# Four graph layers over 32 batches on one core: first loads put in another order, weights split later, and new places for all stages

## The reference, cut to what matters

```
x = L0(x): q,k,v = x@Wq.T+bq, x@Wk.T+bk, x@Wv.T+bv       (8 heads)
           s = q.k/sqrt(32), -inf where adj + eye == 0
           x = layernorm(x + softmax(s) v @ Wo.T + bo)*gamma+beta
x = L1(x): q,k,v as above with its weights                (8 heads)
           s = q.k/sqrt(32) + a_i + c_j + log(adj+1e-9)
           x = x + softmax(s) v          (no output projection)
x = L2(x): f = x@W_fc+b ; logits = (f@w_q)_i + (f@w_k)_j  (one head)
           masked by adj, leaky relu, softmax, x = x + att @ f
x = L3(x): like L0 with log(max(adj,1e-8)) in place of the mask
```

## Time and profile before

| what | us |
|---|---|
| median of 3 runs | 1794.17 |
| the 3 runs | 1792.88 to 1796.88 |
| the profiled execution, whole | 1796.79 |
| its span, first to last instruction | 1795.0 |
| first group, layer 0, 8.1 to 141.8 us | 133.7 |
| second group, layer 0, 448.2 to 576.3 us | 128.1 |
| layers 1, 2, 3 of the second group | 117.0, 76.5, 112.0 |

### The profile page before, as it was taken

How to read it: one execution, slowest core, us unless ns; L and a number is a source line. 1 busy time by engine, 2 the same in 40 slices (tenths; PEclk the granted TensorE clock), 3 DMA queues, 4 the chain that set the end, 5 groups by cost and what they waited for, 6 DMA issues and landing times.

```text
span 1795.0 us, 53987 instructions
## 1 busy us (share of the span) xinstructions
PE 1684.0 (94%) x23308; PEld 1290.8 (72%) x23308; DVE 1371.3 (76%) x2556; ACT 1203.0 (67%) x1886; POOL 1330.2 (74%) x994
## 2 busy tenths in 40 slices
PE   4899999899999999889999999989999999998996
PEld 3677776787776777677777677767777777766874
DVE  2899777767699976776779987776778998777674
ACT  2567875467877786456877787546687778754675
POOL 3555799278977499638987759945898767992788
PEclk8999999999999999999999999999999999999998
DMA  7100010102121001100222100010123200101001
GB/s 217 43 19 19 16 29 25 36 14 66 55 89 49 18 15 37 31 19 19 74 82 66 37 19 20 27 47 7 31 73 94 61 19 14 32 25 36 14 26 42
DMA packets 76432, 74.79 MB, mean 42 GB/s; under 512 B 6562, under 2 KB 76196, under 8 KB 76196
## 3 DMA queue, kind: packets, MB, share of 16 engines
q1 hardware_dynamic: 75092, 70.55, 13.2%
q10 hardware_dynamic: 1104, 0.79, 0.1%
HBM read 62.93 MB, written 8.39 MB: 40 GB/s over the span
## 4 chain that ended last, share of the span: by engine, by line
PE 78%; DVE 9%; POOL 5%; ACT 3%; issue 3%; SPq 2%; DMA 1%; DVEq 0%; POOLq 0%; ACTq 0%
PE gx L640 23%; PE sc L738 18%; PE od L780 17%; PE gx L792 6%; PE sc L744 3%; PE sc L732 3%; PE gx L828 3%; PE gx L665 2%; ACT ring L906 1%; DVE negm L999 1%; PE gx L758 1%; DVE xs L1088 1%; DVE lg L1070 1%; DVE parts L999 1%; POOL xs L632 1%
## 5 line engine op out<-in xcount | busy, mean ns | idle before, releaser
L625 POOL TENSOR_TENSOR ring<-ring,adj_c 128x1024 f32<-128x1024 f32 x256 | 605.4, 2397 | 11.1 <-ACT ring L906 8.7
L738 PE MATMUL sc<-qk 32*128 32x256 f32 x9216 | 410.5, 294 | 31.2 <-DVE negm L999 11.1
L738 PEld LDWEIGHTS sc<-qk 32*128 32x128 f32 x9216 | 320.5, 184 | 135.6 <-issue 76.2
L888 ACT ACTIVATE aside<-sc 128x1024 f32<-128x1024 f32 x192 | 196.7, 1024 | 166.2 <-PE sc L738 113.3
L906 ACT ACTIVATE ring<-sc 128x1024 f32<-128x1024 f32 x256 | 248.3, 1023 | 49.9 <-PE sc L744 49.4
L780 PE MATMUL od<-ring,vf 128*32 128x256 f32 x3072 | 243.3, 388 | 7.0 <-issue 5.0
L780 PE MATMUL od<-ring,halves 128*32 128x256 f32 x3072 | 237.3, 380 | 0.0
L999 DVE TENSOR_REDUCE parts<-sc 128x4 f32<-128x1024 f32 x128 | 156.6, 1223 | 98.3 <-PE sc L738 96.8
L598 POOL TENSOR_TENSOR xs<-xs,bo 128x512 f32<-128x512 f32 x96 | 128.8, 1342 | 120.5 <-DVE xt_lo L969 120.1
L1026 DVE TENSOR_TENSOR ring<-ring,adj_c 128x1024 f32<-128x1024 f32 x128 | 182.2, 1464 | 0.0
L1002 DVE TENSOR_REDUCE parts<-aside 128x4 f32<-128x1024 f32 x128 | 154.9, 1211 | 16.7 <-ACT aside L888 16.5
(11 more groups left out here) (144 smaller groups left out, 4231.2 us busy)
## 6 DMA issues: line engine op xcount, KB each, us to landing
adj_c<-in_adj_t SPq DMA_DIRECT2D x96, 256.0 KB, 2.8
adj_r<-in_adj SPq DMA_DIRECT2D x64, 256.0 KB, 3.0
x_raw<-in_x_t SPq DMA_DIRECT2D x32, 256.0 KB, 3.4
xs<-in_x SPq DMA_DIRECT2D x32, 256.0 KB, 3.3
out<-xs SPq DMA_DIRECT2D x32, 256.0 KB, 2.2
wo<-in_w_o SPq DMA_DIRECT2D x2, 256.0 KB
ring<-in_w_q ACTq DMA_DIRECT2D x1, 256.0 KB, 3.8
ring<-in_w_k ACTq DMA_DIRECT2D x1, 256.0 KB, 5.1
```

What stands on the lines that cost most here:

```text
L625: pool.tensor_tensor(part, part, adj_c[i.mi % 3][:, t, :].unsqueeze(1).to_broadcast([P, G, N]), ALU.mult).then_inc(weighted, 1)
L738: mm = pe.matmul(sc[:, g, t * N:(t + 1) * N], buf[rows, a, c, t * P:(t + 1) * P], buf[rows, b, c, :], start=(n == 0 and not masked), stop= ...
L888: act.activation(aside[:], sc[:, 0:2, :], ACT.Copy).then_inc(set_aside, 1)
```

## The change

1. SP's start. `adj_r` 1 is loaded fourth, then the small loads, `adj_c` 0, and `xs` of the first two batches only. Everything else comes from the sorted list: `xs` of batches 2 to 7 is now an LX, `adj_r` 2 an LR, `adj_c` 1 and 2 LCs. Behind each of LR 3 to 7 a few loads of those that stood in one block before are put: six of `plain` behind the first two each, the last three of `plain` and q1, k1, v1 behind the third, fc, q3, k3 behind the fourth, v3 behind the fifth.
2. `SPLIT_AT` places the splits of the later layers' weights at 19 to 41 instead of 13 to 26.2.
3. POOL scales the bias of q0 behind `xt_lo` of item 0, and those of q1 and q3 at item 7's PC.
4. All place tables and `PITCH` have new numbers.

The program has the same products; by its list ACT has 122 loads of an activation table where there were 116, since other functions now follow each other.

```diff
-SPLIT_AT = (None, -0.06, -0.05, 13, 15.2, 17.4, 19.6, 21.8, 24, 26.2)
+SPLIT_AT = (None, -0.06, -0.05, 19, 21, 23, 27, 33, 37, 41)
...
 MHA_PLAN1 = {
...
-    "S": {PE: [5.649, 6.16], ACTE: [6.962, 8.435], DVE: [6.511, 7.353]},
+    "S": {PE: [3.965, 5.194], ACTE: [4.851, 6.582], DVE: [4.449, 6.529]},
...
-PITCH = {0: (4.4, 4.65), 1: (4.55, 4.45), 2: (4.65, 4.4), 3: (4.9, 4.95)}
+PITCH = {0: (4.6, 4.55), 1: (4.65, 4.55), 2: (4.9, 4.65), 3: (4.9, 4.85)}
...
             sp.dma_start(x_raw[1][:], x_t_all[items_l0[1].batch]).then_inc(xt_loaded[1], 16)
+            sp.dma_start(adj_r[1][:], adj_all[rows_of[1].batch]).then_inc(adjr_loaded[1], 16)
             for dst, src in fold_plain:
                 sp.dma_start(dst, src).then_inc(w_fold, 16)
-            for i in items_l0[:GROUP]:
+            sp.dma_start(adj_c[0][:], adj_t_all[mha[0].batch]).then_inc(adjc_loaded[0], 16)
+            for i in items_l0[:2]:
                 sp.dma_start(xs[:, i.slot], x_all[i.batch]).then_inc(x_loaded[i.slot], 16)
-                if 0 < i.ar < 3:
-                    sp.dma_start(adj_r[i.ar][:], adj_all[rows_of[i.ar].batch]).then_inc(adjr_loaded[i.ar], 16)
-                if i.mi < 3:
-                    sp.dma_start(adj_c[i.mi][:], adj_t_all[i.batch]).then_inc(adjc_loaded[i.mi], 16)
-            for dst, src in plain:
-                sp.dma_start(dst, src).then_inc(w_plain, 16)
-            for n in range(3, len(WEIGHTS)):
-                load_weight(n)
+
+            def some_later_loads(n):
+                for dst, src in plain[6 * n:6 * n + 6]:
+                    sp.dma_start(dst, src).then_inc(w_plain, 16)
+                if n >= 2:
+                    for m in range(3, len(WEIGHTS))[3 * (n - 2):3 * (n - 1)]:
+                        load_weight(m)
...
+                elif s == "LX" and i.k >= 2:
+                    if i.group:
+                        sp.wait_ge(stored[i.slot], 16 * i.group)
                     sp.dma_start(xs[:, i.slot], x_all[i.batch]).then_inc(x_loaded[i.slot], 16)
...
+                    if 3 <= i.ar < GROUP:
+                        some_later_loads(i.ar - 3)
...
-            pool.wait_ge(w_first, 32)
-            pool.tensor_scalar(b_col["q0"][:], b_col["q0"][:], SCALE, None, ALU.mult).then_inc(cols_set, 1)
...
+                    if i.k == 0:
+                        pool.wait_ge(w_first, 32)
+                        pool.tensor_scalar(b_col["q0"][:], b_col["q0"][:], SCALE, None, ALU.mult).then_inc(cols_set, 1)
...
-                    if i.k == 5:
+                    if i.k == GROUP - 1:
```

More of the change, by code:

```diff
@@ L61 @@
 }
 MHA_PLAN1 = {
[L63 to L67, removed]
-    "S": {PE: [5.649, 6.16], ACTE: [6.962, 8.435], DVE: [6.511, 7.353]},
-    "U": {DVE: [8.017]},
-    "M": {PE: [8.028], ACTE: [9.527]},
-    "E": {PE: [9.902, 11.302], ACTE: [10.866, 13.803], POOL: [10.343, 10.556], DVE: [20.96, 23.698]},
@@ L72 @@
[L72 to L78, removed]
+    "O": {PE: [1.099], ACTE: [2.697], POOL: [-7.232]},
+    "T": {PE: [-4.405], ACTE: [-2.768], DVE: [-3.798]},
+    "Q": {PE: [-1.16], ACTE: [0.904], DVE: [0.309]},
+    "P": {PE: [-0.299], ACTE: [1.066], DVE: [0.559]},
+    "V": {PE: [0.111], ACTE: [1.606], DVE: [85.806]},
+    "S": {PE: [3.965, 5.194], ACTE: [4.851, 6.582], DVE: [4.449, 6.529]},
@@ L79 @@
+    "U": {DVE: [7.665]},
+    "M": {PE: [7.554], ACTE: [8.687]},
+    "E": {PE: [9.001, 10.771], ACTE: [10.454, 13.129], POOL: [3.303, 4.647], DVE: [33.037, 33.662]},
+    "A": {PE: [13.726, 15.202, 15.696, 15.985]},
+    "N": {DVE: [16.978]},
+    "F": {PE: [19.142]},
+    "XB": {POOL: [-7.412]},
+    "H": {DVE: [20.768]},
+    "LC": {SP: [28.654]},
+    "PC": {POOL: [-5.795]},
 }
 MHA_PLAN3 = {
-    "T": {PE: [-6.128], ACTE: [-5.034], DVE: [-6.002]},
-    "Q": {PE: [-0.869], ACTE: [0.837], DVE: [-0.372]},
@@ L83 @@
[L83 to L93, removed]
@@ L94 @@
-    "LC": {SP: [22.274]},
-    "PC": {POOL: [-8.955]},
+    "T": {PE: [-6.385], ACTE: [-4.228], DVE: [-4.981]},
+    "Q": {PE: [-1.351], ACTE: [1.173], DVE: [-0.029]},
+    "P": {PE: [2.168], ACTE: [2.236], DVE: [2.866]},
+    "V": {PE: [2.77], ACTE: [3.292], DVE: [82.769]},
+    "S": {PE: [3.255, 6.592], ACTE: [5.351, 6.716], DVE: [4.291, 7.306]},
+    "U": {DVE: [8.059]},
+    "M": {PE: [7.738], ACTE: [8.381]},
+    "E": {PE: [8.645, 12.018], ACTE: [10.983, 12.772], POOL: [-4.523, -3.382], DVE: [15.453, 16.026]},
@@ L96 @@
+    "A": {PE: [15.425, 15.825, 17.01, 17.035]},
+    "N": {DVE: [17.924]},
+    "F": {PE: [23.974]},
+    "XB": {POOL: [-16.952]},
+    "H": {DVE: [25.165]},
+    "LC": {SP: [4.476]},
+    "PC": {POOL: [-14.151]},
 }
 LN_PLAN0 = {
-    "B": {DVE: [23.449]},
-    "Z": {ACTE: [27.077]},
-    "Y": {DVE: [26.124], ACTE: [29.319], POOL: [27.197]},
+    "B": {DVE: [21.898]},
+    "Z": {ACTE: [25.148]},
+    "Y": {DVE: [25.845], ACTE: [27.221], POOL: [19.701]},
 }
 LN_PLAN3 = {
-    "B": {DVE: [27.746]},
@@ L104 @@
-    "Z": {ACTE: [31.23]},
-    "Y": {DVE: [30.39], ACTE: [34.223], POOL: [24.809]},
+    "B": {DVE: [26.337]},
+    "Z": {ACTE: [27.443]},
+    "Y": {DVE: [29.663], ACTE: [30.585], POOL: [18.415]},
 }
 FIRST_PLAN = {
[L108 to L111, removed]
+    "LT": {SP: [-6.929]},
+    "LX": {SP: [22.309]},
+    "LR": {SP: [-3.496]},
+    "PR": {POOL: [-21.353]},
 }
 LAST_PLAN = {
-    "OUT": {SP: [61.449]},
+    "OUT": {SP: [50.439]},
@@ L115 @@
 }
 GAT_PLAN = {
[L117 to L126, removed]
+    "T": {PE: [-5.849], ACTE: [-4.938], DVE: [-4.935]},
+    "G": {PE: [-4.32, -0.506], DVE: [-2.794, 1.468]},
+    "J": {ACTE: [5.528]},
@@ L127 @@
+    "K": {PE: [5.636]},
+    "L": {DVE: [7.476]},
+    "X": {ACTE: [10.992]},
+    "W": {PE: [12.328], ACTE: [12.954]},
+    "C": {DVE: [14.944], PE: [13.36]},
+    "LR": {SP: [13.058]},
+    "PR": {POOL: [-8.701]},
 }
-PITCH = {0: (4.4, 4.65), 1: (4.55, 4.45), 2: (4.65, 4.4), 3: (4.9, 4.95)}
+PITCH = {0: (4.6, 4.55), 1: (4.65, 4.55), 2: (4.9, 4.65), 3: (4.9, 4.85)}
 GAT_START, LAST_START = 23, 31
```

59 lines of the change are left out of this document (30 added, 29 removed).

## The result

The kernel after took 1774.42 us in the median of 4 runs (1774.19 to 1775.89), the kernel before 1794.95 beside it (1792.88 to 1796.88). The ratio is 0.9887 with a 95% interval of 0.9874 to 0.9900: 20.5 us less, where 27.5 were forecast. That is inside the range of 1752 to 1783 given for 8 in 10, and at the upper edge of the forecast's own, 1758 to 1775. Its profiled execution took 1775.89 us, with a span of 1774.1.

A forecast was written before the change was run, and what follows sets the result against it. PE was taken to bound the kernel, with only some 111 us of idle and slow-clock time to win. Start 17.5 plus steady groups 10 gave 27.5 off the 1794.17 median: 1767, own range 1758 to 1775, 8 in 10 1752 to 1783.

The forecast's parts named there:

- The start: First layer-0 pass: earlier third x and first product, less the later split's cost, gain 17.5 us, between 14 and 23.
- the slow clock and the first product: Start of the first pass: 3.1 us from the slow stretch behind the x wait, 0.9 from PE's first product.
- The clock: PE's granted clock in 30 to 45 us, 0.55 before, was to be near 1.
- The later split: First pass, widening block on DVE: saves 3.9 us at its old place, costs 5.6 at the new, bounds 0 to 9.
- The steady groups: New places in layers 0 to 3 of the groups: 10.1 us gain, taken as 10, carried bounds +20 and -12.
- The 1.7 for both ends of layer 2: Layer 2's entry and exit: of 4.2 us of PE waits a group, 1.7 won, bounds 0 to 3.
- Layer 1: PE's waits for the maximum that frees sc: 1.5 of 2.8 us a group won, bounds -2 to +2.8.
- Layer 0 of the second group: New order in groups 2 to 4: loss of 0.9 us a pass, bounds -4 to +1; second group 128 to 130.
- (a): Rival: only the start gives, the new places trade waits one for one: 1777, chance 0.22.
- (d): Rival: single score buffer in the three score layers meets DVE or ACT too early, slower: 1800, chance 0.05.
- (e): Rival: table loads or layer-1 POOL on the path, or dearest block, 8 to 12 lost: 1775 to 1779, chance 0.05.
- (b): Rival: xs of later batches behind waits in SP's queue, POOL meets six unlanded, 20 us lost: 1787, chance 0.06.

The follow-up runs named there:

- e1_start_only: Kernel before with only the new first loads and POOL's later bias scaling, all places, PITCH and splits old: 1777.04 us, ratio 0.9888.
- e1_again: Same program as e1_start_only, the start alone against the kernel before, run again beside the whole change: 1775.64 us, ratio 0.9894.
- e4: Kernel after with SPLIT_AT of the kernel before, so old splits under the new places: 1789.86 us, ratio 0.9968 to the kernel before.
- r5: e1_start_only with the kernel after's order from the start of each layer 1 to the start of layer 3: 1772.82 us, ratio 0.9880.
- r3: Kernel after with the old order from the second item of each layer 2 to the start of layer 3: 1774.47 us, ratio 0.9879.
- r1: Kernel after with the old order in layer 0 of the second to fourth groups on PE, ACT, DVE and POOL: 1808.23 us, ratio 1.0068.
- r2: e1_start_only with the kernel after's order from the start of each layer 1 to the start of its layer 2: 1788.85 us, ratio 0.9959.

## Why the prediction was right or wrong

**The start: right in its main term, with two smaller ones off.** The forecast was 17.5 of gain at the end of the first pass, 14 to 23; the two profiles of the kernel after have 16.4 and 19.9 (at E1 of item 7). Step by step: x issued at 7.9, measured 7.95; no wait above 3 us, longest 1.8; `pick` unchanged at 1.8. PE's first product came at 7.64 and 7.32 instead of 8.08, 0.4 to 0.8 where I had 0.9. The fourth item's v was to come 19.2 us earlier; measured 16.7 and 18.5 in two profiles, and 17.6 and 17.7 under the old places (e1_start_only, e1_again). As 15.2 of it are the wait, the slow clock and the first product gave 2.4 to 2.5 there, where I had 4.0. The block ahead of the third x was longer than I had written ahead of the prediction: not 20 loads but 23 of biases and weights, and five xs.

**The clock: half right.** I had it near 1 in 30 to 45 us. It was 0.89 against 0.55 before: the wait for `pick`, which ends at 33.7 us, leaves a slow stretch of its own (granted clock 0.57 in 34 to 38 us). The later wait for DVE's maximum, to 41.2 us, leaves none, and in e4 the same wait for `pick` leaves none either (granted clock 1.00 in 30 to 45 us). That the clock differs between executions of one program is below.

**The later split: inside its bounds, but too dear, and its dependence was missed.** I had 5.6 at the new place (a wait of 2.5 to 3, a backlog, a dip of the clock) for 3.9 at the old. PE's wait there is 1.54 us in both profiles, and the slow stretch behind it is in the first alone (0.89 against 1.00 in 90 to 105 us). Neither does the old place always cost its 3.9: e1_again has the wait of 2.4 without a dip. From the start alone to the kernel after, E1 of item 7 shows no loss of 1.7 (17.1 and 19.7 against 16.4 and 19.9). That this term was too dear and the clock's too generous made the 17.5 come out, which is in part luck. (The block moved by an item and a third, not by the two items of the prediction's sentence.) And I weighed it as a term by itself. e4 shows that the old numbers cost 15 us under the new places and nothing under the old.

**The steady groups: the failed step.** "Sum: 4 x (1.5 + 1.7) - 3 x 0.9 = 10.1" came out as 4.5 and 3.5 by the two profiles, from E1 of item 7 to the end of the trace, and as 2.2 by the times, the splits' cost included. The 3.2 a group for layers 1 and 2 were 1.0 to 1.1 in r5. The 1.7 for both ends of layer 2 is the term that wasn't there: its pass has 76.1 us against 76.5, and r3 takes the order at both ends back at no cost. In the second group PE's waits in that layer add up to 6.2 us beside 7.3, and in layer 3 to 5.5 beside 4.4: what the entry gained, the exit lost, the wait at L828, now L836 (C's product; I had called it W's), went from two of 1.1 to one of 1.1 and a small one, and waits for `lg` and `qk` took its place. I had costed the waits that the new order covers, and not the ones that it uncovers at the same spot.

Layer 1 was right in kind: no wait of PE is left in 557.9 to 674.0, of the `negm` waits, 2.8 us in six, one of 0.6 is left, at 697.6 in the next stretch, and the pass has 116.1 us for 117.0, where I had 115.5. Layer 0 of the second group took 128.3, in the 128 to 130 that I gave; PE's waits there rose from 1.6 to 4.7 us. But r5, with the old layer 0, isn't faster than the kernel after, so that this loss by waits isn't a loss in time that these runs could show; by position it may be up to half a us a group. Which stage of layers 0 and 3 makes the waits equal stays open; the two runs that were to show it (r1, r2) measured their seams.

**The rivals.** (a), "only the start gives", at 1777 was nearer to 1774.4 than the forecast's 1767, and the truth lies between them. It had the right reason, waits traded one for one, for layers 0, 2 and 3. Of (d) and (e) there is no sign. (b), loads in a waiting queue, did occur in the kernel after, and PE didn't pay for it. This is POOL's wait for `xs` over the whole trace, total, times, longest, in a place where the kernel before had none:

```profile
POOL xs L606 <- DMA xs<-in_x: 47.6, 14, 6.4
```

Behind the first 40 us no wait of PE in that trace names POOL, so that POOL had room for these; r1 shows what they cost where it has not.

The six more table loads left no mark in the time: the traces count 122 in the kernel after (1773.4) and 116 in r5 (1772.8), level within the intervals, though r5 differs in other things too. A row of the kernel after, in layer 0, again has the next instruction 0.01 us behind the load:

```profile
87.53 1.28 ACT L917 ACT_TABLE_LOAD   x1
88.82 0.29 ACT L917 ACTIVATE std<-mv,eps_col 128x2 f32<-128x2 f32 x1
```

The drain that the Trainium skill adds ("ScalarE: Activation LUTs", section "What ACT_TABLE_LOAD costs") is not in these rows, nor ahead of the load (ACT's instruction before it ends at 87.50 us); the 1283 ns of the load itself is.

## What to carry to other kernels

In a queue that issues in order, sort the first loads by when their first user runs, and read the user's wait back to the issue time: one block of loads moved behind the first five x was worth 17 us here, and moving a single load ahead of it only 7, since the next urgent one stood behind it too. When an order is replanned, cost the waits that the new order opens at the same place as carefully as those that it closes; of 10 us forecast from closed waits 2 to 4.5 came. And change the lists of all engines together: of four mixtures of two plans that are each good, two lost 12 and 34 us at their seams, and two lost nothing.

## What the runs showed that I had not expected

The time of a stretch differs from one execution to the next of the same program. The kernel after in its second profile, for the stretches of the first one above:

```profile
12.00:30.00 18.00, 17.12 (x161) 12.95 (x159) 10.77 (x20) 8.10 (x14) 8.58 (x12) 1.00 0.64 142
30.00:45.00 15.00, 11.28 (x148) 8.99 (x148) 7.72 (x13) 7.85 (x12) 8.45 (x13) 0.89 0.33 103
90.00:105.00 15.00, 14.31 (x203) 10.58 (x196) 14.79 (x28) 10.13 (x16) 7.07 (x6) 1.00 0.04 11
```

At 12 to 30 us the granted clock is 1.00 instead of 0.91 and at 90 to 105 us 1.00 instead of 0.89, and E1 of item 7 comes 3.5 us earlier (161.0 against 164.6), with the same instructions in the same order. In both PE had first idled 7.3 to 7.6 us for its first input and 1.8 us for `pick`. The two profiles of the start alone differ likewise: behind the 2.4 us wait the clock is 0.83 in 58 to 68 us in one and 1.00 in the other. So whether a slow stretch follows a given wait is not settled by the program; what settles it is not shown. It isn't the start alone either: the table has steps of 1.2 to 1.6 us in the fourth group in some profiles of kernels with the old places and not in others. A difference of 2 or 3 us between two single profiles therefore says nothing; the medians of the runs, or a gain that comes again from group to group, do.
